# Queries of the first attention by Strassen's seven products of halves

## The chip, the cores and the metric

The kernel runs on one core of one Trainium2 chip. The metric is the device time of one execution in microseconds. The core has five engines that each run a queue of their own in order and meet at semaphores: TensorE (PE, matrix products into PSUM), VectorE (DVE), ScalarE (ACT), GpSimd (POOL) and SyncE (SP, which here issues DMAs and DMA transposes).

## The reference, cut to what matters

A decoder of two layers, each a cross attention and a feed-forward part, on 2048 tokens (32 sequences of 64) of width 512. The change lies in the first attention, whose queries come from the normalised x and whose keys and values come from the context:

```python
x = x + _L0_xattn_ref(_layernorm(x, axis=-1), ctx_4096, L0_xattn_wq, L0_xattn_wk, L0_xattn_wv, L0_xattn_wo)
...
q = (query @ wq).reshape(b, tq, HQ, D)
k = (key @ wk).reshape(b, tk, HKV, D)
v = (value @ wv).reshape(b, tk, HKV, D)
...
scores = jnp.einsum('bqhd,bkhd->bhqk', q, k)
probs = jax.nn.softmax(scores, axis=-1)
out = jnp.einsum('bhqk,bkhd->bqhd', probs, v).reshape(b, tq, HQ * D)
return out @ wo
```

Here HQ is 32 query heads, HKV 8 key and value heads, D 128; k and v are repeated four times to meet q.

## The kernel before

Every float32 operand of a product is held as two float16 tensors, a high part (ScalarE's rounded copy) and a low part (VectorE's difference). A product takes three passes (`PASSES`: high by high, high by low, low by high).

**Prologue** (lines 377 to 465). Four stages of 512 tokens each. In a stage eight units run: four 128-token tiles of the context, then four of the normalised x. TensorE transposes a tile into PSUM, ScalarE writes the high part (`hi_done`), VectorE the low part (`lo_done`) into CT or XT. GpSimd normalises the x tiles (`XN`) once VectorE and ScalarE have the statistics. Then come the high and low parts of the first group's weights (`high_q`, `high_kv`, `low_q`, `low_kv`), and this block of programs ends.

**Attention** (`attention0`). Eight groups `g` of four query heads with one key and value head; in each, four blocks `t` of 512 tokens. TensorE does in block (g, t), in this order: `scores` of the block; `project` of the *next* block, units 0 to 3 (the four heads' queries, 12 matmuls of 512 columns each) and unit 4 (keys); `weigh_values` pair 0 (the first weighting, which needs the transposed probabilities PT); unit 5 (values, 48 matmuls of 128 columns); `weigh_values` pair 1 (the second weighting, which waits until `low_out(0)` has emptied the two banks of the first, `ot_lo`); `project_out`, four pieces of 12 matmuls into two banks `xp`, of which the third and fourth wait for `accumulate` of the first and second (`x_acc`).

Beside it, in the order of their queues:

- VectorE: maxima and difference (`scores_less_max`) of both halves; `sums`, `low(0)`, `normalise`, `sums`, `low(1)`, `normalise`; `low_probs` twice; `low(2)`; in block 0 WO's low part (line 878); `low(3)`; in blocks 2 and 3 `low_weights`; `low(4)` (keys); `low_out(0)`; `low(5)` (values); `low_out(1)`; then four `accumulate` with pieces of the preparation of the next stage's weights between them (maxima and scales in block 0, grid steps of 1024 columns in blocks 1 and 2) and, in block 2, `low_q` and `low_kv` of the next group.
- ScalarE: exponentials with `high(0)` between them; the probabilities' high parts with `high(1)` between (in blocks 2 and 3 also `high_weights`); `high(2)`, `high(3)`; in blocks 1 and 2 eight scalings of prepared weights (line 671); in block 0 four weight DMAs (`load_weights`); `high(4)`; `high_out(0)`; `high(5)`; `high_out(1)`; in block 2 `high_q`, `high_kv`; in block 0 the loads of the next group's weights.
- GpSimd: two operations of 1024 columns for each half of the prepared weights (lines 563 and 565).
- SyncE: two DMA transposes of the probabilities into PT per block (line 534), which wait for `e_hi` and `e_lo`; two of prepared weights in blocks 2 and 3.

In the last group no weights are prepared; pieces of the next stage's normalisation (`x_pieces`: moments, scales, normalised x, maxima, scales) stand in VectorE's queue in its blocks 1 and 2 instead, the first ahead of `low(3)`, the third ahead of `low_out(0)`. The stages behind (first feed-forward, second attention, second feed-forward) are not touched, but for semaphore clears.

## Time and profile before

| | us |
|---|---|
| median of 3 runs | 1642.33 |
| lowest, highest | 1639.29, 1645.27 |
| the profiled execution | 1639.45 |
| its span, first to last instruction | 1637.7 |
| first matmul of the attention | 56.31 |
| first matmul of the next stage | 1010.19 |

The mean granted clock of TensorE is 0.974 of full speed. The profile is one execution; 1.75 us of its own time lie outside the span. A timeline row gives the start, the duration to the last write, the engine, the line, the operation, the tiles and the count, and in brackets the idle time before it with what ended it. Operations overlap a little on an engine: the next one can start up to 0.2 us before the end that is shown for the one ahead, so the time from start to start is the price where an engine is dense.

### The profile page before, as it was taken

The numbers are of one execution on the slowest core, as the hardware profiler recorded it, in microseconds if no ns is written. First come the engines' busy times: TensorE is split into PE (matmuls) and PEld (weight loads), VectorE is DVE, ScalarE is ACT, GpSimd is POOL, SyncE is SP. The second block draws the span as 40 slices with busy tenths as digits, with TensorE's granted clock in tenths as the row PEclk, the third lists the DMA queues.
The fourth block names the chain that finished last, engine by engine and source line by source line (L and its number), as shares of the span: only waits on it lengthen the run. The fifth ranks groups of instructions, "written<-read, shape, count | busy, mean of one in ns | idle before, by whom it ended". The sixth has DMA issues, their size and how long they took to land. (4 is left out here: it accounts for less than half of the span.)

```text
span 1637.7 us, 29866 instructions
## 1 busy us (share of the span) xinstructions
PE 1493.0 (91%) x11323; PEld 795.2 (49%) x11323; DVE 1250.3 (76%) x2330; ACT 831.1 (51%) x1757; POOL 267.8 (16%) x245
## 2 busy tenths in 40 slices
PE   5799999999999999999999986799999987787695
PEld 4455555555555555555555542344445544343353
DVE  6577667668677667767776786799999985999777
ACT  3433434424334243343333332888989864888652
POOL 2001002001011011011011000001111103889620
PEclk9899999999999999999999998899999999999898
DMA  7022231322313222221321123122223250867402
GB/s 270 1 78 52 67 90 27 79 77 44 100 39 59 85 58 59 65 65 53 78 52 53 37 93 117 24 46 46 45 47 64 59 97 1 149 107 121 78 1 103
DMA packets 274122, 114.06 MB, mean 70 GB/s; under 512 B 239184, under 2 KB 255696, under 8 KB 273744
## 3 DMA queue, kind: packets, MB, share of 16 engines
q1 hardware_dynamic: 235104, 79.26, 23.1%
q10 hardware_dynamic: 38896, 33.03, 6.3%
q8 instruction: 94, 1.54, 0.4%
q14 instruction: 28, 0.23, 0.0%
HBM read 45.15 MB, written 11.53 MB: 35 GB/s over the span
## 5 line engine op out<-in xcount | busy, mean ns | idle before, releaser
L583 PE MATMUL pj<-XT,WQ 128*128 128x512 f16 x1536 | 338.5, 380 | 6.4 <-PEq L377 6.4
L625 PE MATMUL xp<-WO,OT 128*128 128x512 f16 x1536 | 340.9, 382 | 3.7 <-DVE X L822 3.7
L625 PEld LDWEIGHTS xp<-WO,OT 128*128 128x128 f16 x1536 | 148.2, 98 | 187.5 <-issue 16.5
L583 PEld LDWEIGHTS pj<-XT,WQ 128*128 128x128 f16 x1536 | 148.5, 98 | 181.6 <-DVE WKV L292 6.6
L822 DVE SCALAR_TENSOR_TENSOR X<-xp,X 128x512 f32<-128x512 f32 x128 | 88.2, 690 | 114.9 <-PE xp L625 114.9
L1027 PE MATMUL db<-W0T,XD 128*128 128x448 f16 x768 | 152.2, 359 | 23.2 <-DVE XD L1226 23.2
L707 ACT ACTIVATE E<-E 128x512 f32<-128x512 f32 x64 | 40.1, 627 | 262.3 <-DVE E L799 262.3
L563 POOL TENSOR_TENSOR VW<-VW,XB 128x1024 f32<-128x1024 f32 x14 | 33.0, 2358 | 757.7 <-DVE VW L105 757.7
L1042 PE MATMUL eb<-W1T,DT 128*128 128x512 f16 x672 | 147.7, 379 | 4.1 <-DMA DT<-HL 2.2
L764 DVE SCALAR_TENSOR_TENSOR QT<-pj,QT 128x512 f16<-128x512 f32 x128 | 87.8, 686 | 55.4 <-ACT QT L686 55.4
L1027 PEld LDWEIGHTS db<-W0T,XD 128*128 128x128 f16 x768 | 75.8, 99 | 98.2 <-DVE XD L1226 23.7
L686 ACT ACTIVATE QT<-pj 128x512 f16<-128x512 f32 x128 | 75.8, 592 | 83.6 <-PE pj L583 83.5
L1042 PEld LDWEIGHTS eb<-W1T,DT 128*128 128x128 f16 x672 | 65.6, 98 | 80.3 <-issue 2.4
L588 PE MATMUL pj<-WKV,CT 128*128 128x128 f16 x1536 | 91.3, 219 | 0.9 <-DVE QT L764 0.9
L588 PEld LDWEIGHTS pj<-WKV,CT 128*128 128x128 f16 x1536 | 85.9, 98 | 7.8 <-issue 6.3
L773 DVE TENSOR_TENSOR OT<-tv,OT 128x512 f16<-128x512 f32 x128 | 82.2, 684 | 8.7 <-ACT OT L695 6.0
L583 PE MATMUL pj<-CT,WKV 128*128 128x512 f16 x384 | 88.1, 379 | 0.0
L695 ACT ACTIVATE OT<-tv 128x512 f16<-128x512 f32 x128 | 69.4, 595 | 19.6 <-PE tv L614 19.6
L1089 ACT ACTIVATE VD<-DB,drec 128x128 f32<-128x128 bf16 x224 | 67.2, 387 | 23.2 <-DVE drec L83 23.2
L712 ACT ACTIVATE EH<-E 128x512 f16<-128x512 f32 x64 | 40.3, 630 | 70.5 <-DVE E L811 70.5
L1409 POOL TENSOR_TENSOR CT<-CT 128x512 f16<-128x512 f32 x64 | 72.6, 1161 | 16.4 <-ACT CT L1639 16.3
L1096 ACT ACTIVATE VD<-VD,dscale 128x128 f32<-128x128 f32 x224 | 68.6, 389 | 11.6 <-DVE VD L1222 11.6
(228 smaller groups left out, 2397.2 us busy)
## 6 DMA issues: line engine op xcount, KB each, us to landing
W0T<-in_L_xattn_wq ACTq DMA_DIRECT2D x7, 1024.0 KB, 5.2
W0T<-in_L_xattn_wo ACTq DMA_DIRECT2D x7, 1024.0 KB, 5.1
CS<-in_ctx SPq DMA_DIRECT2D x4, 1024.0 KB, 10.1
X<-in_x SPq DMA_DIRECT2D x4, 1024.0 KB, 11.2
out<-X SPq DMA_DIRECT2D x8, 512.0 KB, 3.6
XB<-in_L_ffn_W ACTq DMA_DIRECT2D x28, 128.0 KB, 2.7
w0t<-XB ACTq DMA_DIRECT2D x7, 512.0 KB, 3.3
w1t<-W0T ACTq DMA_DIRECT2D x7, 512.0 KB, 3.8
```

The costliest lines, as they stand in the source:

```text
L583: last = pe.matmul(bank[:, :], w, src[:, b, k, tokens], start=n == 0, stop=n == 3 * KC - 1)
L588: last = pe.matmul(bank[:, i * P:(i + 1) * P], CT[:, a, k, own], WKV[:, b, k, 1, :], start=n == 0, stop=n == 3 * KC - 1)
L625: last = pe.matmul(xp[i % 2][:, :], OT[:, a, j, i * P:(i + 1) * P], WO[:, b, j, :], start=n == 0, stop=n == 3 * REP - 1)
L686: act.activation(QT[:, 0, :, u, :], q_bank(u), ACT.Copy, scale=UNSCALE).then_inc(S["pj_hi"], 1)
L695: act.activation(o_out(0, pair, h), o_bank(h), ACT.Copy).then_inc(S["ot_hi"], 1)
L764: dve.scalar_tensor_tensor(out=to[0], in0=q_bank(u), scalar=UNSCALE, in1=to[1], op0=ALU.mult, op1=ALU.subtract).then_inc(S["pj_lo"], 1)
L773: dve.tensor_tensor(o_out(1, pair, h), o_bank(h), o_out(0, pair, h), ALU.subtract).then_inc(S["ot_lo"], 1)
L822: dve.scalar_tensor_tensor(out=xt, in0=xp[i % 2][:, :], scalar=UNSCALE, in1=xt, op0=ALU.mult, op1=ALU.add).then_inc(S["x_acc"], 1)
L1027: last = pe.matmul(db[q][:, 0:NQ], XD[:, i[1] % 2, a, k, :], W0T[:, b, k, q * NQ:(q + 1) * NQ], start=False, stop=n == 3 * KC - 1, skip_gr ...
L1042: last = pe.matmul(eb[:, :], DT[:, a, c, :], W1T[:, b, c, :], start=False, stop=c == IC - 1 and (a, b) == PASSES[-1], skip_group_check=True)
L1096: last = act.activation(VD[:, r, c, :], VD[:, r, c, :], ACT.Copy, scale=ds_[:, r, c:c + 1])
L1409: pool.tensor_tensor(EH[:, 1, q, :], E[:, q, :, :].rearrange("p u n -> p (u n)"), EH[:, 0, q, :], ALU.subtract).then_inc(S["e_lo"], 1)
```

## The change

The queries of a block are a product of 512 tokens by 512 inputs by 512 outputs (four heads). They are now computed by the Strassen-Winograd scheme on halves: seven products of 256 by 256 by 256 per block, each 12 matmuls of 256 columns, on seven sets of x (`XR`, sums of halves of the normalised x) and seven sets of weights (`WQ`, of which four are sums). Three of them add into a bank that already holds another (`Q_BANKS`).

- TensorE: `query_products` 0 to 4 (products 1 to 5), keys, products 6 and 7, first weighting, values, second weighting. Products use the banks `xp` too.
- VectorE: five `add_query` and one `low_query` instead of `low(0)` to `low(3)`; ScalarE: `first_query` and four `high_query`; GpSimd: three `low_queries` per block.
- Weights: `scale_q` on ScalarE and `sum_q` on GpSimd in block 1; `high_q` (3584 columns for 2048), `low_q` on VectorE (1536 for 2048) and `low_q_sums` on GpSimd (2048) in block 2.
- Prologue: 11 units per stage for 8 (four of the context, seven sets), and four sums per stage on GpSimd. The sets of each stage are written to DRAM and read back for every block by SyncE's queue (`load_sets`, five sets and then two).
- The semaphores of the attention are cleared on SyncE in the next stage.

```diff
+SETS = 7
+HALF = BLOCK // 2
+A11, A12, A22, S1, S2, S3, S4 = range(SETS)
+Q_WEIGHTS = (A11, S2, S1, A12, S3, A22, S4)
+B11, T2, T1, B21, T3, T4, B22 = range(SETS)
+SET_WORDS = 2 * 2 * HALF
...
+        def scale_q(act, g):
+            act.wait_ge(W["sq_ld"], g * 16 + 16)
+            act.activation(SQ[:, :, :], SQ[:, :, :], ACT.Copy, scale=WEIGHT_SCALE).then_inc(W["qkv_hi"], 1)
+        def sum_q(pool, g):
+            if not (isinstance(g, int) and g == 0):
+                pool.wait_ge(W["qs_lo"], g)
+            pool.wait_ge(W["qkv_hi"], g * 5 + 1)
+            pool.tensor_tensor(TW[:, 0], weight_block(1, 0), weight_block(1, 1), ALU.add).then_inc(W["q_sums"], 1)
+            pool.tensor_tensor(TW[:, 2], weight_block(0, 0), weight_block(1, 0), ALU.subtract).then_inc(W["q_sums"], 1)
+            pool.wait_ge(W["q_sums"], g * 4 + 1)
+            pool.tensor_tensor(TW[:, 1], TW[:, 0], weight_block(0, 0), ALU.subtract).then_inc(W["q_sums"], 1)
+            pool.wait_ge(W["q_sums"], g * 4 + 3)
+            pool.tensor_tensor(TW[:, 3], weight_block(0, 1), TW[:, 1], ALU.subtract).then_inc(W["q_sums"], 1)
...
+            act.wait_ge(W["q_sums"], g * 4 + 4)
+            to, source = first_columns(0)
+            act.activation(to, source, ACT.Copy).then_inc(W["qkv_hi"], 1)
+            act.activation(WQ[:, 0, A22, :, :], weight_block(1, 1), ACT.Copy).then_inc(W["qkv_hi"], 1)
+            act.activation(WQ[:, 0, S1:, :, :], TW[:, :, :, :], ACT.Copy).then_inc(W["qkv_hi"], 1)
...
+            dve.wait_ge(W["qkv_hi"], g * 5 + 2)
+            to, source = first_columns(1)
+            dve.tensor_tensor(to, source, first_columns(0)[0], ALU.subtract).then_inc(W["qkv_lo"], 1)
+            dve.wait_ge(W["qkv_hi"], g * 5 + 3)
+            dve.tensor_tensor(WQ[:, 1, A22, :, :], weight_block(1, 1), WQ[:, 0, A22, :, :], ALU.subtract).then_inc(W["qkv_lo"], 1)
+        def low_q_sums(pool, g):
+            pool.wait_ge(W["qkv_hi"], g * 5 + 4)
+            pool.tensor_tensor(WQ[:, 1, S1:, :, :], TW[:, :, :, :], WQ[:, 0, S1:, :, :], ALU.subtract).then_inc(W["qs_lo"], 1)
...
+                for i in range(BLOCKS):
+                    sp.wait_ge(lo_done, unit_end(i, PER - 1))
+                    sp.dma_start(set_rows(i, 0, SETS), staged[i].rearrange("p s h c n -> p (s h c n)")).then_inc(W[f"xset_st{i}"], 16)
+                    if i == 2:
+                        sp.wait_ge(W["xset_st2"], 16)
+                        load_o(sp, 0)
...
+                    pool.tensor_tensor(TX[:, 0], far_x[:, :, left], near_x[:, :, left], ALU.subtract).then_inc(tx_ready, 1)
+                    pool.tensor_tensor(TX[:, 1], far_x[:, :, right], far_x[:, :, left], ALU.subtract).then_inc(tx_ready, 1)
+                    pool.wait_ge(tx_ready, blk * 4 + 1)
+                    pool.tensor_tensor(TX[:, 2], far_x[:, :, right], TX[:, 0], ALU.subtract).then_inc(tx_ready, 1)
+                    pool.wait_ge(tx_ready, blk * 4 + 3)
+                    pool.tensor_tensor(TX[:, 3], near_x[:, :, right], TX[:, 2], ALU.subtract).then_inc(tx_ready, 1)
+                    if blk == 2:
+                        sum_q(pool, 0)
+                low_q_sums(pool, 0)
...
+        Q_BANKS = (pj[0], pj[1], xp[1], pj[0], xp[0], xp[0], xp[1])
...
+                    if g < GROUPS - 1 or t < SPG - 2:
+                        sp.wait_ge(S["pt_done"], n_of(g, t, 32, 32))
+                        for lo, hi in ((0, 5), (5, SETS)):
+                            sp.wait_ge(S["qp_done"], n_of(g, t + 1, SETS, hi))
+                            load_sets((t + 2) % SPG, lo, hi)
...
+            def low_queries(g, t):
+                for n in range(3):
+                    pool.wait_ge(S["q_hi"], n_of(g, t, 4, n + 2))
+                    i, j, buffer = ((1, 1, 1), (1, 0, 0), (0, 1, 2))[n]
+                    pool.tensor_tensor(queries(1, i, j), query_sum(buffer), queries(0, i, j), ALU.subtract).then_inc(S["q_lo"], 1)
+            def group(g, last):
+                for t in range(SPG):
+                    nxt = (g, t + 1) if t < SPG - 1 else (g + 1, 0)
+                    if not (last and t == SPG - 1):
+                        low_queries(*nxt)
+                    if last:
+                        continue
+                    if t == 1:
+                        sum_q(pool, g + 1)
+                    if t == SPG - 2:
+                        low_q_sums(pool, g + 1)
...
+            def query_products(g, t, which):
+                first = isinstance(g, int) and g == 0 and t == 0
+                for n in which:
+                    if n == 0:
+                        pe.wait_ge(S["qkv_lo"], g * 3 + 3)
+                        pe.wait_ge(S["qs_lo"], g + 1)
+                        if not first:
+                            pe.wait_ge(S["xr_ld"], n_of(g, t, 32, 0))
+                            pe.wait_ge(S["kv_lo"], n_of(g, t, 2, 0))
+                    elif n == 2 and not first:
+                        pe.wait_ge(S["x_acc"], n_of(g, t, 4, 1 - 4))
+                    elif n == 3:
+                        pe.wait_ge(S["q_first"], n_of(g, t, 1, 1))
+                    elif n == 5:
+                        pe.wait_ge(S["q_add"], n_of(g, t, 5, 2))
+                    elif n == 6:
+                        pe.wait_ge(S["q_add"], n_of(g, t, 5, 3))
+                    fresh = n in (0, 1, 2, 4)
+                    for m in range(2):
+                        for step, (c, (a, b)) in enumerate([(c, ab) for ab in PASSES for c in range(2)]):
+                            last = pe.matmul(head_columns(Q_BANKS[n], m), WQ[:, a, Q_WEIGHTS[n], c, m * P:(m + 1) * P],
+                                             XR[:, n, b, c, :].rearrange("p (b t) -> p b t", b=4), start=fresh and m == 0 and step == 0, stop=step == 5, skip_group_check=True)
+                    last.then_inc(S["qp_done"], 1)
...
+            def project_keys(g, t):
+                pe.wait_ge(S["q_add"], n_of(g, t, 5, 1))
...
+            def project_values(g, t):
+                pe.wait_ge(S["q11_lo"], n_of(g, t, 1, 1))
...
+                pe.wait_ge(S["q_lo"], n_of(g, t, 3, 3))
...
                     if i >= 2:
-                        pe.wait_ge(S["x_acc"], n_of(g, t, 4, i - 1))
+                        pe.wait_ge(S["x_acc"], n_of(g, t, 4, i))
+                    elif more:
+                        pe.wait_ge(S["q_add"], n_of(g, t, 5, 5 + 4 + i))
...
                         scores(g, t)
+                    early = True
                     if more:
-                        project(*nxt, range(4))
-                    if more:
-                        project(*nxt, (4,))
+                        query_products(*nxt, range(5))
+                        project_keys(*nxt)
+                        if early:
+                            query_products(*nxt, (5, 6))
+                        else:
+                            project_values(*nxt)
                     weigh_values(g, t, 0)
                     if more:
-                        project(*nxt, (5,))
+                        if early:
+                            project_values(*nxt)
+                        else:
+                            query_products(*nxt, (5, 6))
                     weigh_values(g, t, 1)
...
+            def first_query(g, t):
+                act.wait_ge(S["qp_done"], n_of(g, t, SETS, 1))
+                act.activation(QA[:, 0, :], pj[0][:, :], ACT.Copy, scale=UNSCALE).then_inc(S["q_first"], 1)
+            def high_query(g, t, n):
+                if n == 0:
+                    act.wait_ge(S["qp_done"], n_of(g, t, SETS, 4))
+                    act.activation(queries(0, 0, 0), query_bank(pj[0]), ACT.Copy, scale=UNSCALE).then_inc(S["q_hi"], 1)
+                else:
+                    act.wait_ge(S["q_add"], n_of(g, t, 5, n + 2))
+                    i, j, buffer = ((1, 1, 1), (1, 0, 0), (0, 1, 2))[n - 1]
+                    act.activation(queries(0, i, j), query_sum(buffer), ACT.Copy).then_inc(S["q_hi"], 1)
...
+                            first_query(*nxt)
                     for jp in range(2):
                         act.wait_ge(S["p_done"], n_of(g, t, 2, jp + 1))
                         act.activation(EH[:, 0, jp, :], E[:, jp, :, :].rearrange("p b k -> p (b k)"), ACT.Copy).then_inc(S["e_hi"], 1)
                         if more and jp == 0:
-                            high(*nxt, (1,))
+                            high_query(*nxt, 0)
                             for p in prepared(t - 1, last):
                                 high_weights(g, *p)
+                    early = True
                     if more:
-                        high(*nxt, range(2, 4))
+                        high_query(*nxt, 1)
                     for p in prepared(t, last):
                         weights_times_rec(g, *p)
                     if last and t in (1, 2):
...
                     if t == 0 and not last:
                         load_weights(act, g)
                     if more:
-                        high(*nxt, (4,))
+                        high_keys(*nxt)
+                        if early:
+                            high_query(*nxt, 2)
+                            high_query(*nxt, 3)
+                        else:
+                            high_values(*nxt)
                     high_out(g, t, 0)
                     if more:
-                        high(*nxt, (5,))
+                        if early:
+                            high_values(*nxt)
+                        else:
+                            high_query(*nxt, 2)
+                            high_query(*nxt, 3)
                     high_out(g, t, 1)
...
+            def add_query(g, t, n):
+                done, bank, other, to = ((2, pj[1], 0, 2), (5, xp[0], 2, 1), (3, xp[1], 1, 1), (6, xp[0], 2, 0), (7, xp[1], 2, 2))[n]
+                dve.wait_ge(S["qp_done"], n_of(g, t, SETS, done))
+                if n == 0:
+                    dve.wait_ge(S["q_first"], n_of(g, t, 1, 1))
                 else:
-                    dve.scalar_tensor_tensor(out=V[:, t % 2, 1, :, :], in0=v_bank(), scalar=UNSCALE, in1=V[:, t % 2, 0, :, :],
-                                             op0=ALU.mult, op1=ALU.subtract).then_inc(S["pj_lo"], 1)
+                    dve.wait_ge(S["q_add"], n_of(g, t, 5, 2 if n == 2 else 1))
+                dve.scalar_tensor_tensor(out=QA[:, to, :], in0=bank[:, :], scalar=UNSCALE, in1=QA[:, other, :],
+                                         op0=ALU.mult, op1=ALU.add).then_inc(S["q_add"], 1)
...
                     scores_less_max(g, t, 1)
+                    early = True
+                    if more:
+                        add_query(*nxt, 0)
                     for jp in range(2):
                         sums(g, t, jp)
-                        if more:
-                            low(*nxt, jp)
                         normalise(g, t, jp)
                     low_probs(g, t, 0)
+                    if more:
+                        low_query(*nxt)
                     low_probs(g, t, 1)
                     if more:
-                        low(*nxt, 2)
+                        add_query(*nxt, 1)
                     if t == 0:
                         dve.wait_ge(S["o_hi"], g + 1)
                         dve.scalar_tensor_tensor(out=WO[:, 1, :, :], in0=SO[:, :, :], scalar=WEIGHT_SCALE, in1=WO[:, 0, :, :],
...
                     if last and t == SPG - 2:
                         first_x[1](dve)
                     if more:
-                        low(*nxt, 3)
+                        add_query(*nxt, 2)
                     x_ahead(1)
                     for p in prepared(t - 1, last):
                         low_weights(g, *p)
                     if more:
-                        low(*nxt, 4)
+                        low_keys(*nxt)
+                        if early:
+                            add_query(*nxt, 3)
+                            add_query(*nxt, 4)
+                        else:
+                            low_values(*nxt)
                     x_ahead(2)
                     low_out(g, t, 0)
                     if more:
-                        low(*nxt, 5)
+                        if early:
+                            low_values(*nxt)
+                        else:
+                            add_query(*nxt, 3)
+                            add_query(*nxt, 4)
                     low_out(g, t, 1)
```

## Rows read from the trace of the kernel before

**Rows 1.** The page, section 1: busy time, share of the span, instructions.

```profile
PE 1493.0 (91%) x11323; PEld 795.2 (49%) x11323; DVE 1250.3 (76%) x2330; ACT 831.1 (51%) x1757; POOL 267.8 (16%) x245
```

**Rows 2.** Timeline of TensorE, one block: start us, duration us, engine, line, operation, tiles, count.

```profile
336.41 1.56 PE L597 MATMUL sc<-KT,QT 128*128 128x64 f16 x48
337.81 10.52 PE L583 MATMUL pj<-XT,WQ 128*128 128x512 f16 x48
348.17 2.75 PE L583 MATMUL pj<-CT,WKV 128*128 128x512 f16 x12
350.86 0.83 PE L614 MATMUL tv<-PT,V 64*128 64x256 f16 x12
351.62 2.85 PE L588 MATMUL pj<-WKV,CT 128*128 128x128 f16 x48
354.40 0.83 PE L614 MATMUL tv<-PT,V 64*128 64x256 f16 x12
...
365.54 1.56 PE L597 MATMUL sc<-KT,QT 128*128 128x64 f16 x48
```

**Rows 3.** Timeline of ScalarE, same columns, blocks 0 and 1 of that group.

```profile
319.39 1.44 ACTq L544 DMA_DIRECT2D XB<-in_L_ffn_W  x2
321.00 1.06 ACTq L547 DMA_DIRECT2D XB<-in_L_ffn_W  x2
...
348.87 2.43 ACT L671 ACTIVATE VW<-XB,wrec 128x128 f32<-128x128 bf16 x8
351.20 0.58 ACT L688 ACTIVATE KT<-pj 128x512 f16<-128x512 f32 x1
```

**Rows 4.** Timeline of VectorE, the same two blocks.

```profile
317.89 2.28 DVE L878 SCALAR_TENSOR_TENSOR WO<-W0T,WO 128x2048 f16<-128x2048 f32 x1
...
346.46 0.68 DVE L764 SCALAR_TENSOR_TENSOR QT<-pj,QT 128x512 f16<-128x512 f32 x1
...
351.81 0.69 DVE L764 SCALAR_TENSOR_TENSOR KT<-pj,KT 128x512 f16<-128x512 f32 x1 [2.12 <-ACT KT L688]
352.42 1.28 DVE L773 TENSOR_TENSOR OT<-tv,OT 128x512 f16<-128x512 f32 x2
```

**Rows 5.** Timeline of SyncE's queue, blocks 1 and 2; then the tile PT.

```profile
345.85 2.58 SPq L534 DMA_TRANSPOSE PT<-EH  x2
...
375.68 2.58 SPq L534 DMA_TRANSPOSE PT<-EH  x2
...
DMA to landing us min/median/max: 2.7/2.8/3.5
```

**Rows 6.** Timelines of VectorE and GpSimd where the two overlap.

```profile
371.54 0.98 DVE L811 TENSOR_TENSOR E<-E,ST 128x512 f32<-128x512 f32 x1
...
370.08 1.90 POOL L565 TENSOR_TENSOR VW<-VW,wscale 128x1024 f32<-128x1024 f32 x1
...
967.04 0.90 DVE L167 TENSOR_SCALAR ln_work<-ln_work 128x4 f32<-128x4 f32 x1
...
966.87 1.05 POOL L241 TENSOR_TENSOR VW<-VW,xscale 128x512 f32<-128x512 f32 x1
```

**Rows 7.** Groups by line, GpSimd: busy us, mean ns | idle before.

```profile
L1409 POOL TENSOR_TENSOR CT<-CT 128x512 f16<-128x512 f32 x64 | 72.6, 1161 | 16.4 <-ACT CT L1639 16.3
...
L415 POOL TENSOR_SCALAR XN<-X,rstd,nmr 128x512 f32<-128x512 f32 x16 | 12.3, 772 | 35.2 <-DVE nmr L172 32.7 <-PE p_tp L432 2.2
```

**Rows 8.** The prologue: timelines of VectorE and TensorE.

```profile
19.70 2.46 DVE L149 BATCH_NORM_STATS2 bn<-X 128x6 f32<-128x512 f32 x4
...
30.27 2.46 DVE L149 BATCH_NORM_STATS2 bn<-X 128x6 f32<-128x512 f32 x4
...
56.31 12.24 PE L583 MATMUL pj<-XT,WQ 128*128 128x512 f16 x48 [6.36 <-PEq L377]
```

**Rows 9.** The last group: timeline of TensorE.

```profile
972.01 1.46 PE L614 MATMUL tv<-PT,V 64*128 64x256 f16 x12 [3.06 <-DVE OT L773]
```

**Rows 10.** The page, section 6: DMA issues, KB each, us to landing.

```profile
W0T<-in_L_xattn_wq ACTq DMA_DIRECT2D x7, 1024.0 KB, 5.2
```

308 lines of the change are left out of this document (195 added, 113 removed).

## The prediction

> **What bounds the kernel now.** I read the page's busy times first: TensorE is busy 91% of the span, the others far less [rows 1]. The timeline of TensorE shows why this stage moves only with it: block follows block without a gap, seven pieces each, 29.13 us from scores to scores (365.54 less 336.41) [rows 2]. Counted from the start of the scores ("s"): queries s+1.40 to s+11.76, keys to s+14.45, first weighting, values from s+15.21, second weighting at s+17.99, and 11.14 us from there to the next scores (the weighting and `project_out`). I then read the other engines against s, since a dense TensorE says nothing of how late the others may be. VectorE's and ScalarE's timelines give the pieces that the change reorders [rows 3, 4]. SyncE's queue shows that the first weighting is nearly held today: its two transposes start at s+9.44 in block 1 and s+10.14 in block 2 (s is 29.13 later), the second is issued 1.3 us after the first (half of 2.58) and lands 2.8 us later, at s+13.5 and s+14.2, against a weighting at s+14.45 [rows 2, 5]. So 0.2 to 0.9 us of slack is all there is in front of it.
>
> **TensorE's own work.** Removed per block: 48 matmuls of 512 columns, 10.36 us, 216 ns each [rows 2]. Added: 84 of 256 columns. No row has this form with 128 rows; half a 512-column one is 108 ns, twice a 128-column one (2.79 us / 48 = 58 ns, values) is 116 ns [rows 2]. I take 109, nearer the first, as per-instruction extra is 2 to 5 ns in both; 84 x 109 = 9.16 us, so a block's queries could give back 1.2 us (0.6 to 1.3). A weight load for every matmul costs nothing visible: scores load one per 64 columns and take 1.40 us / 48 = 29 ns [rows 2]. Here a rule speaks against the change. The Trainium skill (TensorE: Matmul & The Clock Gate, Back-to-back issue gap) gives 81 ns sustained for 128 columns and 131 ns for 512; between them a 256-column matmul would be near 98 ns by my estimate, and 84 of them would cost 1.9 us more than 48 of 131. The rows disagree with both ends (58 and 216 ns); the measurement decides and the sum doesn't use it.
>
> **What the seven products add around it.** Per block VectorE gets 5 `add_query` and one `low_query` for 4 lows, ScalarE 5 copies for 4, each 0.6 us apart [rows 4]; GpSimd gets 3 `low_queries` of 1.16 us [rows 7]. In busy time that fits. In order it doesn't. ScalarE must now take `high_query(1)`, which waits for `add_query` 2, before its weights and `high_keys`; then `high_query` 2 and 3, which wait for `add_query` 3 and 4, before `high_out(0)`; and VectorE runs `low_keys`, `add_query` 3, 4 before `low_out(0)`. The second weighting waits for that. From the start of `high_keys`, call it h: copy 0.60, `low_keys` 0.60, `add_query` 3 0.60 and 4, the copies `high_query` 2 (h+2.0) and 3 (h+2.6), `high_out(0)` h+3.1 and h+3.6 to h+4.2, last `low_out` h+4.3 to h+5.0. So the second weighting can't start before **h+5.1**. Before, the keys' copy at 351.20 was followed by the second weighting 3.20 us later, of which OT's lows ended 0.7 us earlier [rows 2 to 4].
>
> Now h, block by block. TensorE's own plan is first weighting at 1.40 + 9.16 + 2.68 = s+13.24 and second at s+16.8.
> - `add_query` 2. Before, the third low ended at 346.46+0.68 = s+10.73 in block 1 [rows 4]. Four such operations instead of three now precede it (`add_query` 0, `low_query`, 1, 2), one short wait less: ends s+11.2.
> - **Block 1 (t=1)**: ScalarE copies s+11.2 to 11.7, then eight weight scalings 2.33 us (351.20-348.87) [rows 3]: h = 14.1, second weighting s+19.1. Block: 19.1+11.14 = 30.2, +1.1.
> - **Block 0**: WO's low, 2.28 us [rows 4], lies between `add_query` 1 and 2, which ends at s+13.3. Product 7 waits for it, first weighting s+14.6. ScalarE: copy at 13.3, four weight DMAs hold its queue 2.67 us (319.39 to 322.06) [rows 3]: h = 16.5, second weighting s+21.6, block 32.7, +3.6.
> - **Block 2**: VectorE starts 0.4 late (a 1024-wide grid step ahead of the maxima), h = 14.5, second weighting s+19.6, block 30.7, +1.6.
> - **Block 3**: no scalings: h = 12.2 lets the second weighting go at its own time; the first is held by the transposes. They start 0.6 us earlier than before (one low less ahead of them), s+9.6, and land at s+13.7. Second weighting 13.7+3.55 = s+17.2, block 28.4, -0.8.
>
> Sum of a group: +1.1+3.6+1.6-0.8 = **+5.5 us**.
>
> **A hold between VectorE and GpSimd.** In block 2, `low_q_sums` is one GpSimd instruction of 2048 elements: 4 x 1.16 = 4.6 us [rows 7]. It starts about s+25, when VectorE has grid steps and `low_kv` to do ahead of the last two `accumulate`. Two rows show what happens then: a VectorE operation of 0.68 us began at 371.54 and ended at 372.52, 0.98 us, one work time behind the end of a GpSimd one (371.98); and a 0.17 us one begun at 967.04 ended at 967.94, where GpSimd's ended at 967.92 [rows 6]. So the wait lasts to the end of the whole instruction. Then one grid step or `low_kv` waits up to 4.6 us, of which, by my layout of its queue, about 1.3 us fall into idle time; the next block's maxima, or `project_out`'s third piece, come some 3.2 us late (0 to 4.6). **+3.2 us a group.** The Trainium skill (SBUF — State Buffer, SBUF: two separate sides) has this as an exclusive lock on a port pair, held for the full instruction; the trace agrees in its two cases, none as long as 4.6 us.
>
> **Seven full groups**: 7 x (5.5+3.2) = +61. **Last group**: block 0 without weight DMAs: h = 13.8, +0.9. Blocks 1 and 2 have the moments (2.46 us and a few small ones, about 2.9) [rows 8] between `add_query` 1 and 2 and the normalising of x between `add_query` 4 and `low_out(0)`; before, one such stall was 3.06 us [rows 9]; I get about +3.1 each. Sum +7.
>
> **Prologue.** A stage is 10.57 us now (30.27-19.70), held by VectorE [rows 8]. It gets 11 units for 8 (+1.8 us on VectorE) and a chain on GpSimd: 4 normalisings of 0.77 and 4 sums of about 1.2 [rows 7], then transpose, copy, subtract and scales: 3.1+4.8+3.2, with the moments in between about 12.7. Three stages +6.3; the last stage's sums end later than its x tiles did (+4); then high and low parts of seven sets: ScalarE 3.3 and GpSimd 4.6, 7.9 against about 5.4 now (a copy of 1.9, then lows of 2.3 and 1.2 by WO's rate [rows 4]). First product near 69.5 instead of 56.31 [rows 8]: **+13**, 10 to 17. First block: two products less, then `add_query`, copy and GpSimd's last low with nothing beside them, and a set load just in time: **+2**.
>
> **Loads.** 1.75 MB of sets per block are issued on SyncE's queue once the transposes have landed, 14 to 15 us ahead of use. 1 MB lands in 5.2 us [rows 10], so about 9 us: hidden, 5 us to spare. Without that cover each block would lose what is missing. The transposes of prepared weights behind them have a block's time. The clears moved into the next stage lie beside its first transposes and cost nothing I can place.
>
> **Sum** against the profiled execution's own 1639.45 us: +61+7+13+2 = +83, 1722.5. The median of the runs is 2.9 us above that execution: 1725.
>
> **Rivals.**
> 1. *The hold stays small* (GpSimd's instruction is let through between VectorE's steps, or ends in VectorE's idle time): 7 x 3.2 = 22 us less, 1703. For it: no row shows a GpSimd instruction of this length, nor who goes first of two that wait; against: the two holds [rows 6].
> 2. *Only part of the ladder is late.* Were the copies quicker to follow each other, or one stall hidden by the other, half of +5.5 and of the last group's would go: 1680 at most, with the hold 1665 to 1700.
> 3. *Faster, the change as meant*: TensorE stays the bound. It needs h at or below s+11.7 in every block (16.8-5.1), where I find 12.2 to 16.5. Then 32 x 1.2 = 38 us come off, and prologue and first block give 15 back: 1642-23 = 1619. For it: TensorE alone is dense today and no engine is over 76% busy; against it: the order of waits, which busy shares don't show.
> 4. *The sets come late*: were they to take 18 us, with weights loading beside them, the first product would wait 4 us in each block: 1725+31 x 4 = 1850.
>
> **How the numbers follow.** Forecast 0.48; hold small 0.22; part of the ladder 0.14; faster 0.09; sets late 0.03; nothing changes (gain and ladder cancel, within 0.3%, about what a measurement of this kernel can tell from no change) 0.02; worse by longer holds, up to 1750, 0.02. The range takes in the first three cases with the bounds of prologue (-3, +4) and hold (0 to 4.6 a group, -22 to +10): 1678 to 1745. Faster 0.09, same 0.02, slower 0.89.
>
> **What would show it.** Right: TensorE idle ahead of the second weighting, released by OT's lows, in blocks 0 to 2 (about 3.4, 2.3, 2.3 us) and not in block 3; product 7 waiting about 1.4 us in block 0; the products' 84 matmuls in 9.2 us; periods of 32.7, 30.2, 34 and 28.4 us; in blocks 2 a VectorE step of several us beside `low_q_sums`; first product near 69.5. Wrong: blocks of 28 us; products far over 109 ns; TensorE waiting for the sets; VectorE steps of normal length beside GpSimd.

## The result, with the profile after

The changed kernel takes 1766.45 us (median of 4 runs, 1761.02 to 1774.86) against 1641.95 us beside it: ratio 1.076, 95% interval 1.071 to 1.082. It is slower, as forecast, but by 124 us where the prediction had 83, and 21 us above the upper end of its range. The profiled execution took 1761.28 us, 5 us under that median, with a span of 1759.6 us, 121.9 more than before's 1637.7; all that is read below comes from it.

The page, section 1, answers to [rows 1]: TensorE's share fell from 91% to 85%, though its busy time is nearly the same (1501.0 us for 1493.0). It got gaps.

```profile
PE 1501.0 (85%) x12523; PEld 922.6 (52%) x12523; DVE 1338.3 (76%) x2414; ACT 879.7 (50%) x1825; POOL 482.2 (27%) x397
```

TensorE's timeline, first two blocks of the second group (columns as in [rows 2]). The idle time ahead of an instruction and what ended it stand in brackets.

```profile
217.25 0.49 PE L776 MATMUL sc<-KT,QT 128*128 128x64 f16 x11
221.30 1.38 PE L776 MATMUL sc<-KT,QT 128*128 128x64 f16 x37 [3.56 <-issue]
222.49 4.33 PE L749 MATMUL pj<-XR,WQ 128*128 128x256 f16 x24
...
236.02 1.48 PE L749 MATMUL xp<-XR,WQ 128*128 128x256 f16 x12 [1.32 <-DVE QA L990]
237.43 0.83 PE L793 MATMUL tv<-PT,V 64*128 64x256 f16 x12
238.19 2.85 PE L765 MATMUL pj<-WKV,CT 128*128 128x128 f16 x48
243.98 0.83 PE L793 MATMUL tv<-PT,V 64*128 64x256 f16 x12 [2.93 <-DVE OT L1011]
...
255.11 1.56 PE L776 MATMUL sc<-KT,QT 128*128 128x64 f16 x48
256.51 2.78 PE L749 MATMUL pj<-XR,WQ 128*128 128x256 f16 x24
...
268.42 0.83 PE L793 MATMUL tv<-PT,V 64*128 64x256 f16 x12
...
274.29 0.83 PE L793 MATMUL tv<-PT,V 64*128 64x256 f16 x12 [2.26 <-DVE OT L1011]
```

Three waits of these two blocks were in the prediction: the product behind `add_query` 2 (1.32 us), and the second weighting behind OT's lows (2.93 and 2.26 us). One was not: at 217.74 TensorE stops 11 products into the scores, for 3.56 us, and what ends it is "issue", so nothing that the profile shows as a wait. The 24 products behind it then take 4.33 us where the same 24 take 2.78 us a block later. The windows of those stretches (columns: window, length, PE busy, instructions, granted clock, DMA share, GB/s) show the clock falling behind the stop to 0.62 on average, so in good part at the 1.2 GHz level, and back at 2.4 GHz from 226.6 on:

```profile
213.00:217.20 4.20, 4.18 (x20) 1.00 0.60 173
217.70:221.30 3.60, 0.04 (x3) 1.00 0.20 71
...
222.50:226.60 4.10, 4.10 (x28) 0.62 0.00 0
226.60:231.00 4.40, 4.40 (x40) 1.00 0.00 0
```

What TensorE waited for in the eight groups, up to 1120 us (in total, times, longest):

```profile
PE tv L793 <- DVE OT L1011: 61.0, 25, 4.8
PE xp L749 <- DVE QA L990: 20.1, 23, 3.9
PE sc L776 <- issue: 18.2, 7, 3.6
PE xp L806 <- DVE X L1060: 17.8, 8, 2.4
```

The lengths of the blocks, from one block's scores to the next, by group (before: 29.13 each, 83.3 for the last group's three):

| group | block 0 | block 1 | block 2 | block 3 |
|---|---|---|---|---|
| predicted | 32.7 | 30.2 | 34.0 | 28.4 |
| first | 34.24 | 30.31 | 33.31 | 28.66 |
| second to fifth | 37.0 to 37.9 | 30.3 | 33.3 | 28.4 to 28.6 |
| sixth, seventh | 37.2, 36.9 | 31.9 | 34.9, 34.8 | 29.3, 28.5 |
| last | 29.96 | 36.59 | 27.51 | |

The whole difference of the spans: first product 71.57 for 56.31 (+15.3), first block +1.8, seven groups 910.5 for 816.4 (+94.1), last group's three blocks 94.1 for 83.3 (+10.7), all that follows 664.3 in both. Together that is the 121.9.

### The profile page after: what moved, and what is told of

Same layout as the page of the kernel before. It is cut to its first block and busy times, and to the rows that moved or that the text cites. A ratio compares the mean times of both kernels' runs of the same rounds, so it can differ in the third digit from the quotient of the medians.

```text
span 1759.6 us, 33213 instructions
## 1 busy us (share of the span) xinstructions
PE 1501.0 (85%) x12523; PEld 922.6 (52%) x12523; DVE 1338.3 (76%) x2414; ACT 879.7 (50%) x1825; POOL 482.2 (27%) x397
## 5 line engine op out<-in xcount | busy, mean ns | idle before, releaser
L806 PE MATMUL xp<-WO,OT 128*128 128x512 f16 x1536 | 356.1, 393 | 19.7 <-DVE X L1060 19.7
L700 POOL TENSOR_TENSOR QT<-QA,QT 128x512 f16<-128x512 f32 x96 | 113.9, 1200 | 635.8 <-ACT QT L884 635.8
L749 PE MATMUL xp<-XR,WQ 128*128 128x256 f16 x1536 | 186.7, 274 | 20.3 <-DVE QA L990 20.1
L749 PEld LDWEIGHTS xp<-XR,WQ 128*128 128x128 f16 x1536 | 147.6, 98 | 52.8 <-DVE QA L990 35.9
L1288 PE MATMUL db<-W0T,XD 128*128 128x448 f16 x768 | 152.2, 359 | 22.9 <-DVE XD L1487 22.9
L749 PE MATMUL pj<-XR,WQ 128*128 128x256 f16 x1152 | 141.3, 279 | 9.7 <-PEq L421 9.7
L884 ACT ACTIVATE QT<-QA 128x512 f16<-128x512 f32 x96 | 59.5, 630 | 143.6 <-DVE QA L990 143.6
L749 PEld LDWEIGHTS pj<-XR,WQ 128*128 128x128 f16 x1152 | 113.2, 100 | 24.8 <-DVE WKV L334 10.1
L793 PE MATMUL tv<-PT,V 64*128 64x256 f16 x768 | 56.5, 283 | 64.5 <-DVE OT L1011 61.0
L1551 POOL TENSOR_TENSOR VW<-VW,xscale 128x512 f32<-128x512 f32 x15 | 15.6, 1041 | 278.3 <-DVE VW L1459 271.4
L990 DVE SCALAR_TENSOR_TENSOR QA<-xp,QA 128x512 f32<-128x512 f32 x128 | 85.0, 684 | 1.4 <-PE xp L749 0.6
```

Source lines behind the costliest of these rows:

```text
L700: pool.tensor_tensor(queries(1, i, j), query_sum(buffer), queries(0, i, j), ALU.subtract).then_inc(S["q_lo"], 1)
L749: last = pe.matmul(head_columns(Q_BANKS[n], m), WQ[:, a, Q_WEIGHTS[n], c, m * P:(m + 1) * P], XR[:, n, b, c, :].rearrange("p (b t) -> p b ...
L806: last = pe.matmul(xp[i % 2][:, :], OT[:, a, j, i * P:(i + 1) * P], WO[:, b, j, :], start=n == 0, stop=n == 3 * REP - 1)
L884: act.activation(queries(0, i, j), query_sum(buffer), ACT.Copy).then_inc(S["q_hi"], 1)
L990: dve.scalar_tensor_tensor(out=QA[:, to, :], in0=bank[:, :], scalar=UNSCALE, in1=QA[:, other, :], op0=ALU.mult, op1=ALU.add).then_inc(S["q ...
L1288: last = pe.matmul(db[q][:, 0:NQ], XD[:, i[1] % 2, a, k, :], W0T[:, b, k, q * NQ:(q + 1) * NQ], start=False, stop=n == 3 * KC - 1, skip_gr ...
```

## The experiments

Times are one execution each, with 1641.0 to 1641.7 for the kernel before beside them, except where a ratio is given. A second measure helps throughout, the **clock's cost**: over windows of 2 us of the seven groups, TensorE's busy time times one less the granted clock, summed. It is 0.0 us in the kernel before and 18.1 us in the changed one. It isn't steady: `e2_transposes_ahead` below has nearly the waits of the changed kernel and 25.7 us of it. The changed kernel's own four executions lie between 1761.02 and 1774.86 us, so where a single execution differs from it by less than some 14 us (`e2_transposes_ahead`, `e4_split`, `p1_after_padded`, `p3_after_padded_early`), the total says little, and the reading rests on blocks and waits in the timeline.

**The ladder, `e3_ladder`.** ScalarE's copies of queries 2 and 3 behind `high_out(0)`, VectorE's additions 3 and 4 behind `low_out(0)`:

```diff
                         high_keys(*nxt)
-                        if early:
-                            high_query(*nxt, 2)
-                            high_query(*nxt, 3)
-                        else:
+                        if not early:
                             high_values(*nxt)
                     high_out(g, t, 0)
+                    if more and early:
+                        high_query(*nxt, 2)
+                        high_query(*nxt, 3)
...
                         low_keys(*nxt)
-                        if early:
-                            add_query(*nxt, 3)
-                            add_query(*nxt, 4)
-                        else:
+                        if not early:
                             low_values(*nxt)
                     x_ahead(2)
                     low_out(g, t, 0)
+                    if more and early:
+                        add_query(*nxt, 3)
+                        add_query(*nxt, 4)
```

> The changed kernel with the ladder taken apart: high_query 2 and 3 behind high_out(0) on ScalarE, add_query 3 and 4 behind low_out(0) on VectorE; nothing is added or left out. Theory L (the second weighting waits for that ladder): blocks from 37.4, 30.3, 33.3, 28.4 to about 35, 27.9, 28.4, 31.5 us, TensorE's wait for OT's lows ahead of the second weighting gone but for the last group (61 us in all now), the whole 45 to 52 us less, near 1712. Rival (some other cost of the seven products, for instance slower matmuls or the banks): within 10 us of 1762.

Measured 1693.33, 73 us less than the changed kernel's median (69 in span), and 19 us below what was expected. TensorE's waits in this kernel:

```profile
PE xp L749 <- DVE QA L990: 25.8, 24, 3.9
...
PE sc L776 <- issue: 17.0, 7, 3.2
PE pj L749 <- ACT QA L875: 7.3, 7, 1.0
PE tv L793 <- DVE OT L1011: 7.2, 9, 2.0
...
PE xp L806 <- DVE X L1060: 3.6, 4, 1.6
```

The waits for OT fell from 61.0 to 7.2 us, and block 1 to 27.98 us in every group: the ladder is what held the second weighting. More came off than the ladder: the waits for X went too (17.8 to 3.6), for GpSimd's long instruction, though it still held a step of VectorE for 3.96 us, began 5.6 us behind the start of `project_out` where it had been 4.5, and the last quarter of `project_out` waited in none of the seven groups; and the clock's cost fell from 18.1 to 6.5. The stop inside the scores stayed.

**The other order, `e1_values_first`.** Values ahead of the first weighting, products six and seven between the weightings, ScalarE's and VectorE's queues to match (`early = False` in all three).

> The changed kernel with the order of the kernel before at the weightings: values projected ahead of the first weighting, products six and seven between the weightings, and the copies in ScalarE's and VectorE's queues to match. Strassen's seven products stay. What is left is the change's gain on TensorE without its ladder. Theory (ladder and hold): blocks of about 30.8 (+4.5 of the stop), 28.4, 28.9, 30.9 instead of 33.3 (+4.5), 30.3, 33.3, 28.4, so about 45 us less than the changed kernel, 1715 to 1725. Rival (the order of the weightings costs nothing, the seven products' own additions do): time within 10 us of the changed kernel's 1766.

Measured 1711.01, 55 us less than the changed kernel, a little more than expected. Blocks 1 and 2 take 28.43 and 28.86, both shorter than before's 29.13. Block 1 keeps a wait for OT of 0.43 us, block 2 two small ones (0.46 us for PT, 0.32 for OT); without them both would be near 28.0, which is 1.1 us under 29.13 where the products were to give 1.2. TensorE in block 1 from the values on:

```profile
132.30 2.84 PE L765 MATMUL pj<-WKV,CT 128*128 128x128 f16 x48
135.07 0.83 PE L793 MATMUL tv<-PT,V 64*128 64x256 f16 x12
135.83 2.79 PE L749 MATMUL xp<-XR,WQ 128*128 128x256 f16 x24
139.06 0.83 PE L793 MATMUL tv<-PT,V 64*128 64x256 f16 x12 [0.43 <-DVE OT L1011]
```

So the place of the last two products and of their copies, and not the seven products themselves, cost about 55 of the 124 us.

**The hold, `e4_split`.** `low_q_sums` as four GpSimd instructions of 512 elements for one of 2048:

```diff
-            pool.tensor_tensor(WQ[:, 1, S1:, :, :], TW[:, :, :, :], WQ[:, 0, S1:, :, :], ALU.subtract).then_inc(W["qs_lo"], 1)
+            for i in range(4):
+                last = pool.tensor_tensor(WQ[:, 1, S1 + i, :, :], TW[:, i], WQ[:, 0, S1 + i, :, :], ALU.subtract)
+            last.then_inc(W["qs_lo"], 1)
```

> The changed kernel with low_q_sums on GpSimd as four instructions of 512 elements instead of one of 2048. Theory H (a VectorE instruction of this kind waits until GpSimd's whole instruction is over): the grid step of 4.55 us beside it falls to at most 1.9 us, block 2 from 33.3 to near 31, block 3 up by about 1 us (the last pieces reach into it), the whole about 10 to 13 us less. Rival (VectorE is slowed for as long as GpSimd works at all, in however many instructions): the grid step and its followers lose the same 3.9 us together and the time stays.

VectorE and GpSimd in the changed kernel (first two lines), and in `e4_split` (the last two):

```profile
180.78 4.55 DVE L105 TENSOR_SCALAR VW<-VW 128x1024 uint32<-128x1024 uint32 x1
...
180.16 4.62 POOL L330 TENSOR_TENSOR WQ<-TW,WQ 128x2048 f16<-128x2048 f32 x1 [5.41 <-ACT WQ L315]
```

```profile
180.26 6.93 POOL L331 TENSOR_TENSOR WQ<-TW,WQ 128x512 f16<-128x512 f32 x4 [5.41 <-ACT WQ L315]
...
180.87 1.65 DVE L105 TENSOR_SCALAR VW<-VW 128x1024 uint32<-128x1024 uint32 x1
```

A grid step that takes 0.68 us alone took 4.55, and ended 0.55 us after GpSimd's instruction. In pieces the two engines take turns: the step takes 1.65, GpSimd's four 6.93 us. Not all of VectorE's work is held: the `accumulate` steps beside the four pieces, which read a PSUM bank, took their usual 0.68 us. Block 2 fell from 33.3 to 30.7 us and TensorE's waits for X from 17.8 to 2.6. Yet the time is 1757.51, only 9 us less than the changed kernel's median and 3.8 us less in span. Over the seven groups block 2 gave back 21 us; block 3 took 9 of them (it rose from 28.4 to about 30, and TensorE's waits for QA from 20.1 to 25.9) and block 0 took 8; the clock's cost rose from 18.1 to 22.9. The mechanism is shown; its price, taken alone, is smaller than the wait that it makes.

**The stop: is it the transfers at the edge?** The weights' stores and transposes run at each group's edge, and a fetch of code would stand behind them. `e2_transposes_ahead` issues the transposes of prepared weights ahead of the sets' loads on SyncE's queue, so that the first store is issued at 206.78 us instead of 213.94, 10 us ahead of the edge; `b1_late_stores` is the kernel before with the stores held until TensorE has ended the third of the block's four pieces of `project_out`, so that they run across the edge as in the changed kernel:

```diff
                     if t == SPG - 1 and not last:
+                        act.wait_ge(S["xp_done"], n_of(g, t, 4, 4))
                         store_weights(act, g)
```

> The changed kernel with one edit on SyncE's queue: the DMA transposes of the prepared weights go ahead of the loads of the sets instead of behind them. In the changed kernel block 0 of every group but the first takes 36.9 to 37.9 us, where the layout of the queues gave 32.7; TensorE stops for 3.6 us after 11 matmuls of the scores with nothing in the profile to wait for. Theory A (code fetch behind stores): the late transposes make ScalarE issue the 1 MB of stores of prepared weights at 213.94, so that they are on the DMA engines when TensorE's program jumps back to the loop's start at 217.25 and must fetch code. Then this edit ends the stop: stores several us before the edge, block 0 near 33, the whole some 25 to 30 us less, near 1733. Theory B (the longer loop body makes the fetch late whatever else moves): block 0 stays at 37 to 38 and the whole within 5 us of 1762.

> The kernel before with one edit: ScalarE waits for the third piece of project_out of block 3 before it issues the two stores of prepared weights (1 MB), so that they run across the loop's edge. Theory A: TensorE, which never stops there in the kernel before (29.12 us a block), now stops some 3 us inside the first scores of a group, and the whole is 20 to 35 us longer, near 1670. Theory B: no stop, and at most 5 us more, from ScalarE's WO copy that follows the stores.

`e2_transposes_ahead` measured 1765.32, and the stop is there with no store on the DMA engines: 2.47 us for 3.56.

```profile
217.18 0.49 PE L776 MATMUL sc<-KT,QT 128*128 128x64 f16 x11
220.15 2.13 PE L776 MATMUL sc<-KT,QT 128*128 128x64 f16 x37 [2.47 <-issue]
```

`b1_late_stores` measured 1645.33 and has no stop at all. The transfers lengthen the stop by 1.1 us at this edge (over all six, 17.5 us against 15.5); they don't make it.

**The stop: is it where the loop's code lies?** TensorE always stops after the same 11 matmuls, in each group but the first, so behind the loop's jump back. With their weight loads these are 22 instructions. The theory: if code comes in blocks, and the next block begins there, the jump lands too close ahead of it for the fetch to be hidden. Then the stop can be moved by instructions ahead of the loop that do nothing. `p1_after_padded` puts 148 waits that are satisfied already (74 instructions as built) there; `p2_before_padded` puts 364 (182 instructions) into the kernel *before*, so that its loop begins as close ahead of such a place.

```diff
             pe.sem_inc(S["xp_done"], 1)
+            for i in range(148):
+                pe.wait_ge(S["xp_done"], 1)
```

> The changed kernel with 148 waits that are already satisfied put into TensorE's queue ahead of its loop (74 instructions in the built program), where TensorE stands idle in the prologue; nothing else is changed. They only move the place of the loop's first instruction within the code. Theory C (TensorE's stop behind the loop's jump is a fetch of code: the jump lands some 22 instructions ahead of the end of a block of code, and the next block comes too late; a longer way to the next boundary hides the fetch): the stop of 3.6 us in the first scores of each group goes, and the stretch at the lower clock behind it; first blocks of the groups fall from 37.4 to about 33, time about 1735 to 1742. Rival B (the stop comes from the longer loop body, or from what the other engines and queues do at the edge, wherever the loop lies): the stop stays, time 1762 to 1768.

> The kernel before, with 364 such satisfied waits (182 instructions) ahead of TensorE's loop, so that its loop begins as close ahead of a boundary of the code as the changed kernel's does. Theory C: a stop of 2.5 to 3.6 us, absent in the kernel before, appears in the first scores of every group but the first, with a stretch at the lower clock behind it: 7 x 3 to 4.5 us, time 1662 to 1673. Rival B: no stop, time 1640 to 1646. The waits themselves could cost the prologue up to 5 us where TensorE is not idle for long enough; that would show ahead of the first product and not in the groups.

`p2_before_padded` measured 1683.04, 41 us more than the kernel before, and 10 us above the theory's range, because the waits themselves cost 19.9 us where at most 5 were expected. At the edge of its second group:

```profile
210.63 0.51 PE L597 MATMUL sc<-KT,QT 128*128 128x64 f16 x12
213.32 1.22 PE L597 MATMUL sc<-KT,QT 128*128 128x64 f16 x36 [2.18 <-issue]
```

Six such stops (2.0 to 2.9 us, 15.0 in all) are in a kernel that had none, and differs only in waits ahead of its loop. The view of the DMA engines from 209 to 215 us (GB/s in 40 slices of 0.15 us) shows what moves then: two packets of the queue named "instruction", so of code, and nothing else; the first 0.3 to 0.5 us after the scores began.

```profile
GB/s 0 0 0 0 0 0 0 0 0 0 0 0 0 109 0 0 0 0 0 0 0 0 0 0 0 0 0 0 0 0 0 0 0 0 0 0 109 0 0 0
...
q8 instruction: 2, 0.03, 2.0%
```

The same view of other kernels at the same edge shows such a packet each time (us):

| kernel | scores begin | packet (to 0.1) | next matmul after the stop |
|---|---|---|---|
| `p2_before_padded` | 210.63 | 211.0 | 213.32 |
| changed, stores on the DMA engines | 217.25 | 218.9 | 221.30 |
| `e2_transposes_ahead`, no stores | 217.18 | 217.5 | 220.15 |
| before | 190.78 | 191.4 | no stop |
| `b1_late_stores` | 192.91 | 195.2 | no stop |

Where TensorE stops, it goes on 2.2 to 2.7 us behind the packet. With the stores gone the packet comes 0.3 us after the scores' begin instead of 1.6, and the stop is 1.1 us shorter: that is what the transfers add. In `b1_late_stores` the packet is even later, 2.3 us, and nothing stops. The second packet in the view above, at 214.4 us, comes when TensorE has gone on. Of the 43.6 us in span, 19.9 lie ahead of the first scores (182 waits, 110 ns each, in a place where TensorE was awaited after all), 20.4 in the seven groups (stops 15.0, the clock's cost 4.5) and 3.3 behind them.

`p1_after_padded` took the stops away: the first blocks behind a jump take 34.1 to 34.4 us, as in the changed kernel's first group (34.24), where no jump precedes. Waits for issue are 4.2 us for 18.2, and what is left stands ahead of the scores (0.6 to 1.0 us), not inside them. The seven groups take 894.3 us for 910.5. But the time is 1755.01, where 1735 to 1742 was expected: its waits cost 7.8 us ahead of the first scores, and the clock's cost stayed, 16.6 for 18.1. So **`p3_after_padded_early`** puts the satisfied waits at the end of TensorE's queue in the stage before, where it waits 9.7 us anyway.

> The changed kernel with the same 148 satisfied waits, now at the end of TensorE's queue in the stage before, where it waits 9.7 us for the meeting of the engines, so that they cost nothing. Everything else stands where p1_after_padded has it. Theory C: the first product returns to 71.6 us, the first blocks of the groups stay at 34.1 to 34.4 us (37 to 38 in the changed kernel), and the time is p1's 1755 less 7.9, 1745 to 1750. Rival (the 11 us that p1 gained were only a state of the clock, or the waits cost something else): 1753 or more.

Measured 1753.73, by its number the rival's. The timeline sides with the theory and tells why the number doesn't: the first product is at 71.27, block 0 takes 32.67 and 32.57 us in the first two groups, the predicted 32.7.

```profile
217.55 1.57 PE L778 MATMUL sc<-KT,QT 128*128 128x64 f16 x48
218.96 2.79 PE L751 MATMUL pj<-XR,WQ 128*128 128x256 f16 x24
...
230.94 1.48 PE L751 MATMUL xp<-XR,WQ 128*128 128x256 f16 x12 [1.32 <-DVE QA L992]
...
238.99 0.83 PE L795 MATMUL tv<-PT,V 64*128 64x256 f16 x12 [3.02 <-DVE OT L1013]
```

But in most blocks behind, about 1.5 us come back as a stretch at the lower clock, behind the waits of block 2 above all (34.6 to 35.0 us in six of seven groups, for 33.3): the clock's cost is 23.9 us for 18.1. Of 14.8 us of waits for issue taken away, the seven groups kept 9.2, where those of `p1_after_padded` kept 16.2. Two windows of this kernel, around the end of the first group's block 2 (34.76 us, until 188.95):

```profile
180.00:188.00 8.00, 5.59 (x22) 0.87 0.00 0
188.00:192.00 4.00, 4.00 (x65) 0.82 0.00 0
```

**All repairs at once.** `c1_all` joins `e3_ladder`, `e4_split`, `e2_transposes_ahead`, the 148 waits of `p1_after_padded`, and VectorE's low part of WO behind `add_query` 2.

> All repairs in one: the two copies of queries behind the first weighting's rounding and the two additions behind its remainder, the subtraction of weights on GpSimd in four instructions, the output weights' remainder behind the third query, the transposes of prepared weights ahead of the loads of sets on SyncE's queue, and 148 satisfied waits ahead of TensorE's loop. From 1693 with the first of these alone: the stop off the edge takes 7 x 3.5 to 4.5 us more, remainder and hold 7 x 1 to 3: 1640 to 1660 by theory C, 1670 to 1685 by rival B.

Measured 1656.46, in the range of the theory. The seven groups take 114.0 to 115.2 us each, under before's 116.5, the clock's cost is 0.0, and what is left of TensorE's waits there is small:

```profile
PE xp L751 <- DVE QA L994: 5.6, 14, 0.5
PE pj L751 <- POOL WQ L331: 4.4, 7, 0.8
PE sc L778 <- issue: 2.8, 4, 1.1
```

`c2_best` moves the waits to the stage before, lets product two instead of one wait for `low_q_sums`, takes `add_query` 2 ahead of the moments in the last group, and products six and seven ahead of the values in the prologue. `c3_best_unpadded` is the same without the satisfied waits.

> c1_all with the satisfied waits in the stage before (-7.9), the wait for the sums' remainders at product two instead of product one (-0.6 at each group's last block, -4), the query addition for the sixth product ahead of the moments of x in the last group (-1.9 and -3.9 there, of which the last block keeps some 2), and in the prologue products six and seven ahead of the values (-2.7). From 1656.5: 1636 to 1642, so between a tie with the kernel before and 0.4% under it. Rival (what the last group and prologue lose has other causes): 1645 to 1650.

> c2_best without the satisfied waits: TensorE's loop begins again some 20 instructions ahead of a boundary of its code. Theory C: stops of 2.5 to 3.6 us in the first scores of six groups with the lower clock behind them, 18 to 30 us over c2_best. Rival B: within 3 us of c2_best.

`c2_best`: 1642.43 (median of 10), ratio to the kernel before 1.0006, interval 0.9989 to 1.0023. It ties with it, 0.4 us above the range expected. Against before it has first scores at 89.21 for 73.66 us (+15.6), groups 803.5 for 816.4 (-12.9), last group 84.8 for 83.3 (+1.5) and 660.9 for 664.3 behind them (-3.4). `c3_best_unpadded`: 1679.66, 37 us more and 7 above the range of the theory: 28.9 in the groups (issue 15.6 for 3.8, waits for PT 11.8 for 0.6, clock 4.3 for 0.0) and 11.0 spread over the later stages. The six stops are back (2.3 to 2.7 us), and they with the lower clock are 16 us of it. The waits for PT can't be put down to them: the first group, ahead of any jump, has one too (1.91 us at 104.58, block 0 takes 30.53 us for 28.55), and the transposes into PT landed there in 3.9 us instead of 2.8. Those 11 us and the 11 us behind the groups are of this one execution, and their cause stays open.

## Why the prediction was right in direction and wrong in size

- **TensorE's own work: right.** The 12 matmuls of 256 columns of one product take 1.31 us from start to start, 109 ns each, as taken between the halves and doubles of [rows 2]. No weight load showed. The Trainium skill's figures (TensorE: Matmul & The Clock Gate, Back-to-back issue gap), 81 ns for 128 columns and 131 ns for 512, stay off at both ends.
- **The ladder: right, to tenths.** In block 0 the keys' copy starts at 238.94 and the second weighting at 243.98, h+5.04 for h+5.1. Block 1's weightings are at s+13.3 and s+19.2 (predicted 13.24 and 19.1), blocks 1 and 3 took 30.3 and 28.4 (30.2, 28.4) in most groups, block 0 without its stop 32.6 (32.7; first two groups of `p3_after_padded_early`). `e3_ladder` undid it.
- **The hold: right, a little over-sized.** 4.62 us of GpSimd held a step of VectorE for 3.9 us beyond its own 0.68; block 2 took 33.3 for 34.0, and 30.7 without the hold (`e4_split`), just as laid out: the hold is 2.6 us a block and not 3.2. It is longer than both cases of [rows 6], and, as the Trainium skill has it (SBUF — State Buffer, SBUF: two separate sides), lasts the full instruction. That GpSimd's 4.62 us match the 4.6 of the prediction is in part luck: in the prologue, with no VectorE step under way when it began, the same instruction took 4.06 us. `e4_split` shows what the prediction didn't say: removing the hold alone gave 4 us in span, not 22.
- **The loads: right.** 1.25 and 0.5 MB of sets landed in 6.1 and 7.4 us, and TensorE never waited for them.
- **Prologue and first block: +15.3 and +1.8 for +13 and +2.** A stage takes 12.3 us (12.7 predicted). Of the 2.1 us missed (71.57 for 69.5), 1.1 are the same hold, left out here: VectorE's low part of the key and value weights began at 66.71 and ended at 70.95, 1.08 us after GpSimd's low sums, and all engines meet behind it. The other 1.0 us was not traced.

```profile
66.71 4.24 DVE L334 SCALAR_TENSOR_TENSOR WKV<-W0T,WKV 128x1024 f16<-128x1024 f32 x1 [1.44 <-ACT WKV L319]
...
65.81 4.06 POOL L330 TENSOR_TENSOR WQ<-TW,WQ 128x2048 f16<-128x2048 f32 x1 [5.14 <-ACT WQ L315]
```

- **Last group: +10.7 for +7, mis-sized.** Its blocks came out at +0.8, +5.9 and +4.0 for +0.9, +3.1 and +3.1. The second block's stalls are 1.94 and 4.84 us, where one of 3.06 [rows 9] gave +3.1: the moments delay the product behind `add_query` 2 *and*, down the ladder, the second weighting. I added one stall where two follow each other.

```profile
1045.14 1.48 PE L749 MATMUL xp<-XR,WQ 128*128 128x256 f16 x12 [1.94 <-DVE QA L990]
...
1055.01 1.42 PE L793 MATMUL tv<-PT,V 64*128 64x256 f16 x12 [4.84 <-DVE OT L1011]
```

- **The seven groups: +94.1 for +61. Two terms were missing**, and they are the miss. The step that failed is "Seven full groups: 7 x (5.5+3.2)": it priced the loop's blocks as if the code were there and the clock full. The stop behind the jump is 17.5 us in six groups (the seventh wait for issue, 0.67 us, stands ahead of the scores), the clock's cost 18.1: together 35.6 against a miss of 33.1, the 2.5 us left over being blocks a little shorter than predicted. Neither exists in these groups of the kernel before, whose TensorE has no gaps there and whose loop starts elsewhere in its code. That the stop is a matter of place is shown both ways, by `p1` and `p3` that remove it and by `p2` that makes it. That what comes late is a block of code rests on the packets: TensorE goes on 2.2 to 2.7 us behind one, and where the packet is 1.3 us later, TensorE is 1.1 us later. Why an equal packet doesn't stop the kernel before is explained by the theory (it is needed later) and not shown by itself. The Trainium skill (Runtime: NRT & Kernel Launch, Instruction fetch mechanics) states that code comes in blocks of 256 instructions and that a taken branch out of the held window forces a fetch before execution goes on; the traces agree in part, since the six stops follow each jump but stand 22 to 24 instructions behind it and not at it, and they cost 2.0 to 3.6 us each. It also calls the crossing of a block mostly hidden; these traces agree where the loop was moved by 74 instructions, and not at 22 to 24 instructions behind a jump.
- **The clock's part is shown as a size, its rule is not.** The lower level follows waits of TensorE of 2 to 5 us; in the seven groups of the kernel before, `c1_all` and `c2_best`, where no such wait stands inside the loop, the cost is 0.0 us. Which wait brings it down changes from group to group in one execution: in the changed kernel the stop does in the second and third groups only, the wait ahead of block 0's second weighting in the first and the fourth to seventh. So single blocks can't be forecast from here, and some 15 of the 18.1 us stand behind waits that the prediction had.
- **Two sums of the prediction don't come out as written.** Rival 2, half of the ladder's price, is 7 x 2.75 + 3.5 = 23 us, which gives 1702 and only with the hold gone too 1680, where it says "1680 at most". And prologue and hold at their upper bounds give 1739, where the range ends at 1745. The 1766 us measured lie above both all the same.

The two terms don't add up independently: taking 17.5 us of stops out of the changed kernel returned 16.2 us (`p1_after_padded`) and 9.2 us (`p3_after_padded_early`) in the groups, and the difference of these two is the clock's cost, 16.6 against 23.9.

## What to carry to other kernels

A stall in a dense TensorE can cost more than its length: here 99 us of waits for VectorE's OT, QA and X and 17.5 us of stops came with 18 us of lower clock, and removing one wait alone often only moved the clock's share. Look where a loop's jump lands after any change of the code ahead of it: a stop of 2 to 4 us on "issue", after the same few instructions in each pass but the first, points to the place of the loop; here it went with 74 idle instructions, best put where the engine waits anyway. The number matters: 182 of them made the stop in a kernel that had none. And in an engine's queue, what the next block needs shouldn't stand ahead of what this block's critical product needs: moving two copies and two additions took 73 us off.

## What the runs showed of the hardware

- Where a loop's code begins is worth some 1% by itself: 182 waits ahead of an otherwise unchanged loop added 20.4 us to its seven passes, and leaving out 74 added 16 us of stops and lower clock in another kernel. With stores on the DMA engines the stop at one edge was 3.56 us, without 2.47, and the packet of code came 1.3 us later with them.
- Waits that are already satisfied aren't free on TensorE: 106 and 110 ns per instruction of two (7.8 us for 74, 19.9 us for 182).
- A 2048-element GpSimd subtraction held a VectorE step on SBUF until its end (4.55 us for 0.68), and in four pieces the two hold each other: GpSimd took 6.93 us for 4.62 while VectorE's step took 1.65 for 0.68. VectorE's steps that read PSUM took their usual 0.68 us beside the pieces.
